# First attention: where VectorE splits the third part of the next quad's weights

## The chip, the cores and the metric

The kernel runs on one core of a Trainium2 chip. The metric is the device time of one execution in microseconds (us), lower is better. Five things work side by side in the core and meet only at semaphores: TensorE (PE for its matmuls, PEld for its weight loads), VectorE (DVE), ScalarE (ACT), GpSimd (POOL) and the sync engine (SP), which here only issues DMA transfers, one after the other in program order.

## The reference, cut to what matters

Input `x` is (4, 512, 256): four batches of 512 tokens of width 256. The model adds three blocks to it: a first causal self-attention with 16 heads of width 64, a cross attention with 16 heads of width 16, and a two-layer local transformer block. The change touches the first attention alone:

```python
xn = layernorm(x)
q = einsum('ahe,bce->bach', W_Q, xn)
k = einsum('ahe,bce->bach', W_K, xn)
v = einsum('ahe,bce->bach', W_V, xn)
scores = einsum('bach,baCh->bacC', k, q)
masked = where(causal, scores, -1e10)
attn = softmax(masked / sqrt(64), axis=-1)
z = einsum('bacC,baCh->bach', attn, v)
x = x + einsum('aeh,bach->bce', W_O, z)
```

## The kernel before, in words

**Units.** The first attention runs as 32 units, each one pair of heads of one batch. Eight units share one quad of heads (`QUNITS` is 8), and there are four quads (`QUADS` is 4). All engines run the same software pipeline of slots: the slot of unit `u` finishes unit `u` (transposes of the probabilities, weighted values), makes scores and softmax of unit `u + 1`, and projects k, q and v of unit `u + 2`. Slots are numbered `j` = 0 to 7 within a quad. A hardware loop (`Fori`) runs over the first three quads, eight slots in its body, and the last quad is written out behind it.

**Weights of a quad.** One DMA (`quad_weights`, line 514) brings 768 KB, the k, q and v weights of a quad, into one buffer `aw`. Matmuls run on rounded float32 operands and a rest: ScalarE rounds each of the three parts into `aw_hi` (line 783), VectorE writes the rest `aw_lo = aw - aw_hi` (`rest_of_weights_of_quad`, lines 1050 and 1051) and counts semaphore `a_lo` up by one for each part. During quad `c` the parts of quad `c + 1` are made: parts 0 and 1 in slot 5 of VectorE's order, part 2 (the v weights) in slot 6. Three things wait on `a_lo`: TensorE's projections (line 1510 for k and q, line 1520 for v, first used for the new quad at the end of slot 6), and SP, since `aw` may be overwritten only when all three rests are made.

**SP's queue.** SP issues for every unit four 128 KB transfers that copy the halves of the rounded k into both halves of `k2` (`other_half`, lines 551 to 555; the profile calls the tiles k and k_round). It first waits until ScalarE has rounded k (`k_hi`), and TensorE's first scores of the unit wait until all four have landed (`k_both`). Between the eighth unit of a quad and the first unit of the next one the same queue holds the wait for the split weights and the next load:

```python
            with sp.Fori(0, QUADS - 2) as c:
                for j in range(QUNITS):
                    other_half(c * QUNITS + j)
                sp.wait_ge(a_lo, 3 * c + 6)
                quad_weights(c + 2)
            for u in range(NU - 2 * QUNITS, NU):
                other_half(u)
```

This loop runs twice. The k of the unit whose `other_half` comes right behind `quad_weights` is rounded in slot 6, and its scores stand at the start of slot 7. At the start of the kernel the same sequence stands once in straight code: a wait for `a_lo` at 3, `quad_weights(1)`, `other_half(0)`.

**VectorE's slot.** In order: copy of the transposed probabilities 0 (`evac_pT`), masked scores of head 0 (three banks, line 1076, then `negmax`, line 1083), copy 2, masked scores of head 1, copy 4, the rest of k (lines 1065 and 1066), reciprocal of the softmax sums of head 0 (line 1088), reciprocal of head 1, the rest of q (lines 1058 and 1059), copy of z (line 1122). GpSimd multiplies the probabilities of a head by the reciprocal (line 658, four instructions for each head), and TensorE's transposes of head 0 of the next slot (line 1560) wait for the four of head 0.

Of the kernel before, what the change touches and what calls it, by code (L numbers as in the profile page):

```python
# [21 lines left out]
QUNITS = 2 * B  # L22
# [59 lines left out]
def build(nc, a, out, x2_dram):  # L82

    with ExitStack() as ctx:
# [199 lines left out]
        def use_z(u):  # L284
            return 5, 3 * u + 2 + B // 2
# [189 lines left out]
        def wait_full(eng, use):  # L475

            bank, n = use
            eng.wait_ge(full[bank], n + 1)
            return psum[bank]
# [544 lines left out]
        def _(dve):  # L1024
# [24 lines left out]
            def rest_of_weights_of_quad(c, i):  # L1049
                dve.wait_ge(a_hi, 3 * c + (i + 1))  # L1050
                dve.tensor_tensor(aw_lo[:, i], aw[:, i], aw_hi[:, i], ALU.subtract).then_inc(a_lo, 1)

            def rest_of_q(u):

                bank = wait_full(dve, use_q(u))
                dve.wait_ge(q_hi, u + 1)
                dve.tensor_tensor(q2[ADH:P, 0, :], bank[0:ADH, :], q2[0:ADH, 0, :], ALU.subtract)
                dve.tensor_tensor(q2[0:ADH, 1, :], bank[ADH:P, :], q2[ADH:P, 1, :], ALU.subtract)\
                    .then_inc(read[use_q(u)[0]], 1)  # L1060

            def rest_of_k(u):
                bank = wait_full(dve, use_k(u))
                dve.wait_ge(k_hi, u + 1)
                dve.tensor_tensor(k_rest[0:ADH, 0, :], bank[0:ADH, :], k_round[0:ADH, :], ALU.subtract)
                dve.tensor_tensor(k_rest[ADH:P, 1, :], bank[ADH:P, :], k_round[ADH:P, :], ALU.subtract)\
                    .then_inc(read[use_k(u)[0]], 1)

            def masked_scores(u, j, h):

                for k, blocks in enumerate(S_TILES):
                    bank = wait_full(dve, use_s(u, h, k))
                    pass_wait(dve, passed_v)
                    at = 0
                    for i in blocks:
                        ins = dve.tensor_tensor_reduce(  # L1076
                            probs[:, j % 2, h, TRI_AT[i]:TRI_AT[i + 1]], bank[:, at:at + TRI[i]],
                            causal[:, S - TRI[i]:S], 1.0, -3e38, ALU.add, ALU.max, rowmax[:, j % 2, h, i:i + 1])
                        at += TRI[i]
                    ins.then_inc(read[k], 1)  # L1080
                for k in range(3):
                    wait_read(dve, use_s(u, h, k))
                dve.tensor_scalar(negmax[:, j % 2, h, :], rowmax[:, j % 2, h, :], -ADH ** -0.5, None, ALU.mult)\  # L1083
                    .then_inc(s_neg, 1)

            def inverse_sums(u, j, h):
                dve.wait_ge(s_exp, 2 * u + (h + 1))
                dve.reciprocal(rden[:, j % 2, h, :], den[:, j % 2, h, :]).then_inc(s_rden, 1)  # L1088

            def evac_pT(u, n):  # L1090

                h, k = divmod(n, 3)
                bank = wait_full(dve, use_t(u, h, k))
                at = KEYB_AT[T_TILES[k][0]]
                w = sum(KEYB[j] for j in T_TILES[k])
                dve.tensor_copy(pT[:, h, at:at + w], bank[:, 0:w]).then_inc(read[use_t(u, h, k)[0]], 1)

            def attention_slot(u, j, ahead, z, c=None):

                evac_pT(u, 0)  # L1100
                if ahead >= 1:
                    masked_scores(u + 1, j + 1, 0)
                if c is not None and j == QUNITS - 2:
                    rest_of_weights_of_quad(c, 2)
                evac_pT(u, 2)
                if ahead >= 1:
                    masked_scores(u + 1, j + 1, 1)
                evac_pT(u, 4)
                if ahead >= 2:
                    rest_of_k(u + 2)  # L1110
                if ahead >= 1:
                    inverse_sums(u + 1, j + 1, 0)
                if c is not None and j == QUNITS - 3:
                    rest_of_weights_of_quad(c, 0)
                if ahead >= 1:
                    inverse_sums(u + 1, j + 1, 1)
                if ahead >= 2:
                    rest_of_q(u + 2)
                if c is not None and j == QUNITS - 3:
                    rest_of_weights_of_quad(c, 1)  # L1120
                bank = wait_full(dve, use_z(u))
                dve.tensor_copy(z, bank[:, :]).then_inc(read[use_z(u)[0]], 1)
# [37 lines left out]
            with dve.Fori(0, QUADS - 1) as c:  # L1160
                for j in range(QUNITS):
                    z = zT[:, j // 2, :, :].rearrange("p k s -> p (k s)")[:, bass.ds((c * 2 + j % 2) * S, S)]
                    attention_slot(c * QUNITS + j, j, 2, z, c + 1)
            for j in range(QUNITS):
                attention_slot(NU - QUNITS + j, j, QUNITS - 1 - j, zT[:, j // 2, PAIRS - 2 + j % 2, :])
# [777 lines left out]
```

## Time and profile before

| | before |
|---|---|
| median of 3 runs | 1221.88 us (1221.18 to 1222.47) |
| profiled execution | 1221.09 us |
| its span in the trace | 1219.2 us |
| TensorE matmuls busy | 1158.6 us (95%) |
| VectorE busy | 843.6 us (69%) |
| ScalarE busy | 686.5 us (56%) |
| GpSimd busy | 592.3 us (49%) |

All times in the trace count from the start of the span. The first attention lies in the first third of it, and the slots 5, 6 and 7 of the first quad lie at 99 to 136 us. In a timeline a row gives the start, the duration, the engine, the line, the operation with output and inputs, the shapes and a count; in brackets stands how long the engine was idle before it, and what ended that. "In the timeline of SP" rows are DMA issues: the time on the row is the issue, not the transfer.

### The profile page before, as it was taken

The numbers are of one execution on the slowest core, as the hardware profiler recorded it, in microseconds if no ns is written. First come the engines' busy times: TensorE is split into PE (matmuls) and PEld (weight loads), VectorE is DVE, ScalarE is ACT, GpSimd is POOL, SyncE is SP. The second block draws the span as 40 slices with busy tenths as digits, with TensorE's granted clock in tenths as the row PEclk, the third lists the DMA queues.
The fourth block names the chain that finished last, engine by engine and source line by source line (L and its number), as shares of the span: only waits on it lengthen the run. The fifth ranks groups of instructions, "written<-read, shape, count | busy, mean of one in ns | idle before, by whom it ended". The sixth has DMA issues, their size and how long they took to land.

```text
span 1219.2 us, 20487 instructions
## 1 busy us (share of the span) xinstructions
PE 1158.6 (95%) x6672; PEld 887.5 (73%) x6672; DVE 843.6 (69%) x2443; ACT 686.5 (56%) x1696; POOL 592.3 (49%) x648
## 2 busy tenths in 40 slices
PE   5899999999999899998789999999999999999998
PEld 4677777787777776666567787777777778777676
DVE  7777778787877356688999567777675876664541
ACT  2667576667667223453567646647475565573821
POOL 2354544445453322148886664655655646562630
PEclk9999999999999999999999999999999999999999
DMA  7122121312121400010021000000001000002000
GB/s 233 40 49 74 41 52 35 78 35 52 35 53 47 162 18 18 1 61 33 3 89 43 1 1 18 1 1 1 1 18 46 29 2 1 1 5 66 19 27 26
DMA packets 31628, 46.11 MB, mean 38 GB/s; under 512 B 4572, under 2 KB 19632, under 8 KB 31536
## 3 DMA queue, kind: packets, MB, share of 16 engines
q1 hardware_dynamic: 31536, 44.98, 12.9%
q8 instruction: 45, 0.74, 0.3%
q14 instruction: 47, 0.39, 0.1%
HBM read 24.00 MB, written 4.19 MB: 23 GB/s over the span
## 4 chain that ended last, share of the span: by engine, by line
PE 56%; issue 20%; POOL 14%; DVE 7%; ACT 3%; DMA 0%; POOLq 0%; DVEq 0%; ACTq 0%
PE psum L1494 34%; POOL probs L658 14%; PE psum L1754 5%; PE psum L1803 5%; PE psum L1788 4%; PE psum L1770 4%; PE psum L1736 2%; ACT hnT_hi L974 1%; DVE lp L1353 1%; DVE ra L1309 1%; ACT hnT L974 1%; DVE rb L1315 1%; PE psum L1816 1%; DVE ss L1319 1%; DVE stats L1027 1%
## 5 line engine op out<-in xcount | busy, mean ns | idle before, releaser
L658 POOL TENSOR_TENSOR probs<-probs,rden 128x128 f32<-128x128 f32 (+3 forms) x256 | 177.6, 730 | 211.2 <-DVE rden L1088 211.2
L813 ACT ACTIVATE probs<-probs,negmax 128x128 f32<-128x128 f32 (+3 forms) x256 | 140.6, 554 | 22.6 <-DVE negmax L1083 22.6
L944 ACT ACTIVATE lp<-lp,lneg,rn 128x256 f32<-128x256 f32 (+1 forms) x256 | 143.8, 571 | 14.1 <-DVE lneg L1365 13.9
L1076 DVE CUSTOM_DVE_ANT_0 probs<-psum,causal 128x512 f32<-128x512 f32 (+3 forms) x256 | 110.0, 486 | 2.2 <-issue 0.8
L702 POOL TENSOR_TENSOR rn<-ss,neg_half 128x8 f32<-128x8 f32 x64 | 106.5, 1664 | 3.8
L1353 DVE CUSTOM_DVE_ANT_0 lp<-psum,local 128x256 f32<-128x256 f32 (+1 forms) x256 | 84.0, 384 | 25.6 <-PE psum L1754 25.6
L693 POOL TENSOR_TENSOR lp<-lp,lrden 128x768 f32<-128x768 f32 x64 | 95.0, 1484 | 0.0
L1494 PE MATMUL psum<-q,k_rest 128*128 128x256 f32 (+2 forms) x256 | 88.8, 358 | 4.3 <-DVE rowmax L1076 2.9
L1560 PE MATMUL psum<-ident,probs 128*128 128x128 f32 x640 | 91.0, 274 | 1.7 <-POOL probs L658 1.6
L1494 PE MATMUL psum<-w,hid 114*128 114x256 f32 (+1 forms) x384 | 85.5, 379 | 1.1 <-DVE hid L1421 1.1
L1494 PE MATMUL psum<-wqkv_hi,hT_lo 128*128 128x512 f32 x192 | 82.1, 428 | 4.1 <-DVE rb L1315 2.8
L690 POOL TENSOR_TENSOR lp<-lp,lrden 128x128 f32<-128x128 f32 x64 | 26.7, 418 | 118.7 <-DVE lrden L1370 118.7
L698 POOL TENSOR_TENSOR ra<-ra,rb 128x512 f32<-128x512 f32 x32 | 41.0, 1281 | 84.8 <-DVE rb L1315 84.7
L1494 PEld LDWEIGHTS psum<-w,hid 114*128 114x128 f32 (+1 forms) x384 | 72.2, 190 | 11.7 <-DVE hid L1421 1.7
L778 ACT ACTIVATE pT<-psum 128x512 f32<-128x512 f32 (+1 forms) x96 | 49.3, 514 | 55.3 <-PE psum L1560 55.3
L1560 PEld LDWEIGHTS psum<-ident,probs 128*128 128x128 f32 x640 | 74.2, 141 | 6.9 <-POOL probs L658 2.1
L1494 PE MATMUL psum<-hnT_lo,w_hi 128*114 128x512 f32 (+1 forms) x192 | 78.8, 411 | 0.0
L1494 PE MATMUL psum<-q,k 128*128 128x256 f32 (+2 forms) x256 | 78.8, 325 | 0.0
L1576 PE MATMUL psum<-pT,v 128*64 128x256 f32 (+3 forms) x512 | 76.0, 439 | 2.3 <-ACT pT L778 1.7
L931 ACT ACTIVATE sq<-psum 128x512 f32<-128x512 f32 x64 | 38.1, 598 | 70.6 <-PE psum L1494 64.3
L1421 DVE SCALAR_TENSOR_TENSOR hid<-psum,b,gl 114x512 f32<-114x512 f32 (+1 forms) x48 | 36.0, 750 | 59.5 <-PE psum L1494 46.8
L1494 PE MATMUL psum<-wqkv_hi,hT_hi 128*128 128x512 f32 x192 | 76.3, 397 | 0.0
(166 smaller groups left out, 3053.5 us busy)
## 6 DMA issues: line engine op xcount, KB each, us to landing
k<-k_round SPq DMA_DIRECT2D x128, 128.0 KB, 2.3
x<-in_x SPq DMA_DIRECT2D x8, 512.0 KB, 6.3
aw<-in_w_quads SPq DMA_DIRECT2D x4, 768.0 KB, 4.9
w_raw<-in_w SPq DMA_DIRECT2D x2, 1364.0 KB, 7.2
ctxT<-in_ctxT SPq DMA_DIRECT2D x4, 512.0 KB, 3.6
x_scratch<-x SPq DMA_DIRECT2D x4, 512.0 KB, 3.3
x<-x_scratch SPq DMA_DIRECT2D x4, 512.0 KB, 5.5
wqkv_raw<-in_wqkv SPq DMA_DIRECT2D x1, 1536.0 KB, 10.0
```

The source lines that it names most:

```text
L658: ins = pool.tensor_tensor(pr, pr, rden[:, j % 2, h, i:i + 1].broadcast_to([P, TRI[i]]), ALU.mult)
L693: pool.tensor_tensor(pr, pr, r, ALU.mult).then_inc(l_prob, 1)
L702: pool.tensor_tensor(rn[:, m % 2, t, i, :], ss[:, i, :], neg_half[:, 0:FH], ALU.pow).then_inc(l_rn, 1)
L813: ins = act.activation(pr, pr, ACT.Exp, bias=negmax[:, j % 2, h, i:i + 1], scale=ADH ** -0.5, accum_out=den[:, j % 2, h, i:i + 1])
L944: ins = act.activation(pr, pr, ACT.Exp, bias=lneg[:, u % 2, h, w:w + 1], scale=rn[:, m % 2, w, 0, 2 * j + h:2 * j + h + 1], accum_out=lden ...
L1076: ins = dve.tensor_tensor_reduce(probs[:, j % 2, h, TRI_AT[i]:TRI_AT[i + 1]], bank[:, at:at + TRI[i]], causal[:, S - TRI[i]:S], 1.0, -3e38 ...
L1353: ins = dve.tensor_tensor_reduce(lp[:, u % 2, h, lo:hi], bank[:, at:at + hi - lo], local[:, LOC - (hi - lo):LOC], 1.0, -3e38, ALU.add, ALU ...
L1494: ins = mm(dst, lhsT, rhs, start=i == 0, stop=i == len(pairs) - 1, **kw)
L1560: ins = pe.transpose(bank[:, at:at + P], probs[:, j % 2, h, lo:lo + P], ident[:, :])
L1576: ins = mm(bank[rows, c * P:S], v[:, b % 2, c, cols], pT[:, h, KEYB_AT[c]:KEYB_AT[c] + KEYB[c]], start=c == 0, stop=c == T - 1)
L1754: ins = mm(pair[h][:, at:at + n].rearrange("p (w k) -> p w k", k=P), lqT[rows, c, d, :], keys[rows], start=True, stop=True)
L1803: ins = mm(bank[:, i * D:(i + 1) * D], loT[:, FPAIRS - 1 - k, t * P:(t + 1) * P], wo[:, k, :], start=i == 0 and k == 0, stop=i == 1 and k ...
```

## The change

In VectorE's `attention_slot`, slot 6 (`j == QUNITS - 2`) of the first three quads, the call that splits part 2 is taken from its place behind the masked scores of head 0 and put behind the reciprocal of head 0 (and behind the split of part 0, which is made in slot 5 only). The number of instructions is the same, and no other engine's code is changed.

```diff
@@ -1100,8 +1100,6 @@
                 evac_pT(u, 0)
                 if ahead >= 1:
                     masked_scores(u + 1, j + 1, 0)
-                if c is not None and j == QUNITS - 2:
-                    rest_of_weights_of_quad(c, 2)
                 evac_pT(u, 2)
                 if ahead >= 1:
                     masked_scores(u + 1, j + 1, 1)
@@ -1112,6 +1110,8 @@
                     inverse_sums(u + 1, j + 1, 0)
                 if c is not None and j == QUNITS - 3:
                     rest_of_weights_of_quad(c, 0)
+                if c is not None and j == QUNITS - 2:
+                    rest_of_weights_of_quad(c, 2)
                 if ahead >= 1:
                     inverse_sums(u + 1, j + 1, 1)
                 if ahead >= 2:
```

## Rows read from the trace of the kernel before

**Rows 1.** TensorE's timeline, slots 5 to 7 of the first quad: start, duration, work, idle.

```profile
99.13 0.60 PE L1560 MATMUL psum<-ident,probs 128*128 128x128 f32 x4
...
114.37 0.50 PE L1494 MATMUL psum<-q,k_rest 128*128 128x512 f32 x1 [0.38 <-DVE rowmax L1076]
...
122.28 0.38 PE L1494 MATMUL psum<-aw_hi,xnT_lo 128*128 128x256 f32 x1
...
123.79 0.60 PE L1560 MATMUL psum<-ident,probs 128*128 128x128 f32 x4
124.22 0.47 PE L1494 MATMUL psum<-q,k_rest 128*128 128x512 f32 x1
...
135.50 0.60 PE L1560 MATMUL psum<-ident,probs 128*128 128x128 f32 x4
```

**Rows 2.** VectorE's timeline of the same stretch, around the three splits.

```profile
105.52 0.69 DVE L1096 COPY pT<-psum 128x512 f32<-128x512 f32 x1 [0.47 <-PE psum L1560]
...
107.54 0.18 DVE L1088 RECIPROCAL rden<-den 128x4 f32<-128x4 f32 x1
107.63 0.66 DVE L1051 TENSOR_TENSOR aw_lo<-aw,aw_hi 128x512 fp32r<-128x512 f32 x1
...
115.59 0.69 DVE L1051 TENSOR_TENSOR aw_lo<-aw,aw_hi 128x512 fp32r<-128x512 f32 x1
...
118.51 0.69 DVE L1096 COPY pT<-psum 128x512 f32<-128x512 f32 x1
...
120.53 0.18 DVE L1088 RECIPROCAL rden<-den 128x4 f32<-128x4 f32 x1
121.43 0.18 DVE L1088 RECIPROCAL rden<-den 128x4 f32<-128x4 f32 x1 [0.72 <-ACT probs L813]
```

**Rows 3.** SP's timeline at 90 to 130 us: DMA issues around the quad's load.

```profile
116.47 0.35 SPq L514 DMA_DIRECT2D aw<-in_w_quads  x1
118.97 2.39 SPq L554 DMA_DIRECT2D k<-k_round  x4
```

**Rows 4.** DMA issues at 118.9 to 121.5 us: KB each, median us to landing.

```profile
k<-k_round SPq DMA_DIRECT2D x4, 128.0 KB, 2.4
```

**Rows 5.** The load issued at 116.4 to 117.4 us: KB, us to landing.

```profile
aw<-in_w_quads SPq DMA_DIRECT2D x1, 768.0 KB, 4.1
```

**Rows 6.** SP's timeline at the kernel's start, where load and k transfers follow directly.

```profile
18.74 0.33 SPq L514 DMA_DIRECT2D aw<-in_w_quads  x1
19.29 1.17 SPq L554 DMA_DIRECT2D k<-k_round  x2
```

**Rows 7.** DMA issues at 18.7 to 22 us: KB each, median us to landing.

```profile
aw<-in_w_quads SPq DMA_DIRECT2D x1, 768.0 KB, 5.4
k<-k_round SPq DMA_DIRECT2D x4, 128.0 KB, 4.5
```

**Rows 8.** TensorE's timeline at 20 to 44 us: two long waits.

```profile
25.76 0.47 PE L1494 MATMUL psum<-q,k_rest 128*128 128x512 f32 x1 [0.62 <-DMA k<-k_round]
...
37.79 0.36 PE L1494 MATMUL psum<-aw_hi,xnT_lo 128*128 128x256 f32 x1 [4.46 <-DVE k_rest L1066]
```

**Rows 9.** Two windows: busy us (count) of each engine, granted clock, DMA share, GB/s.

```profile
38.30:41.70 3.40, 3.40 (x16) 3.29 (x15) 1.29 (x3) 0.60 (x1) 0.89 (x1) 0.50 0.02 5
550.30:553.70 3.40, 3.40 (x10) 2.63 (x9) 2.56 (x7) 0.60 (x1) 3.22 (x4) 0.50 0.00 0
```

**Rows 10.** TensorE's timeline at 540 to 553 us, its longest wait there.

```profile
549.88 0.50 PE L1494 MATMUL psum<-wqkv_hi,hT_lo 128*128 128x512 f32 x1 [2.56 <-DVE rb L1315]
```

**Rows 11.** GpSimd's timeline, first instruction of a unit: slot 4, then slot 5.

```profile
96.08 0.40 POOL L658 TENSOR_TENSOR probs<-probs,rden 128x128 f32<-128x128 f32 x1 [6.25 <-DVE rden L1088]
...
107.80 0.76 POOL L658 TENSOR_TENSOR probs<-probs,rden 128x128 f32<-128x128 f32 x1 [6.25 <-DVE rden L1088]
```

**Rows 12.** Weight loads' timeline: first transposes of slot 6.

```profile
111.03 0.42 PEld L1560 LDWEIGHTS psum<-ident,probs 128*128 128x128 f32 x4 [0.22 <-issue]
```

## The prediction

> **What bounds the kernel now.** I read TensorE's timeline of the slots around the change first. Its first transposes start slot 5 at 99.13 us, slot 7 at 123.79 and the next quad's slot 0 at 135.50 [rows 1]. Slot 7 takes 11.71 us and shows no wait: the matmuls of a slot run back to back, so in the first attention TensorE sets the pace, and every wait it gets is time of the kernel. Slots 5 and 6, which hold the splits, take 24.66 us together, 1.24 us more than two plain slots. The visible part of that is where TensorE waits in slot 6 for the masked scores (0.38 us at 114.37, more on single weight loads) [rows 1]; it comes before part 2 is split at 115.59 [rows 2], so part 2 does not cause it. Parts 0 and 1, which the change leaves alone, do.
>
> Then VectorE's timeline: where does part 2 lie now? In slot 5, a plain slot at this point, the copy of transposes 4 starts after 0.47 us of waiting for TensorE (105.52). In slot 6 the same copy starts at 118.51 with no wait [rows 2]. So the split of 0.69 us fills a gap of 0.47 us that would be there anyway, and VectorE is late by at most the difference, 0.22 us, because of it; and the second reciprocal of slot 6 waits 0.72 us for ScalarE again, so even that lateness ends on VectorE itself.
>
> Last, SP's timeline, since SP waits for this split. At 116.47, 0.88 us after the split's start, it issues the 768 KB load of the quad after next; only at 118.97 do the four k transfers of the next unit follow, because k is rounded only then [rows 3]. SP had time to spare: 2.5 us between the two.
>
> **The change, part by part.**
>
> *What it takes away.* 0.69 us of VectorE behind the masked scores of head 0, three times. Worth: nothing to 0.22 us each, since the wait for transposes 4 comes back in its place, and the wait for ScalarE behind it stays. I take 0.
>
> *What it adds on VectorE.* The split stands behind the first reciprocal. In slot 5 this very arrangement runs with part 0: reciprocal at 107.54, split at 107.63 for 0.66 us. In slot 6 the first reciprocal starts at 120.53 and the second at 121.43, after 0.72 us of waiting for ScalarE's exponentials [rows 2]. The split would run from 120.62 to 121.28 and fit into the gap with 0.15 us to spare. The second reciprocal, the rest of q and the copy of z stay where they are. TensorE's v projection for the new quad waits for part 2 too; it starts at 122.28 [rows 1], 1.0 us after the split's new end. That cover holds. Cost on VectorE: 0.
>
> *What it adds on GpSimd.* GpSimd starts its multiplications just behind the first reciprocal, and now beside the split. In slot 5 that is so today: the first instruction took 0.76 us instead of 0.40 in slot 4, which has no split [rows 11]. The delay of 0.36 us passes through the four instructions of head 0, for which the first transposes of the next slot wait. After slot 5 they show 0.22 us of waiting (111.03) [rows 12]. From the first reciprocal of slot 5 (107.54) to these transposes it was 3.49 us, with GpSimd as the one waited for. The same distance behind the reciprocal at 120.53 [rows 2] puts the transposes of slot 7 at 124.02 instead of 123.79 [rows 1], 0.23 us later. Bounds: 0, if they keep today's time, and 0.36. I take 0.2. The Trainium skill (SBUF — State Buffer, Who interferes with whom) says that a VectorE instruction with both inputs in SBUF and a GpSimd instruction that reads SBUF exclude each other, and the later one blocks until the first is done. By that rule the delay would be from 107.80, GpSimd's start, to the split's end, 108.29, which is 0.49 us; the row shows 0.36, and the sum would grow by 0.1 us per quad.
>
> *What it moves on SP.* This is the large term. The split's start moves from 115.59 to 120.62, by 5.0 us, and SP's wait with it. The load is then issued at 120.62 + 0.88 = 121.50 in place of 116.47. SP works in order: the four k transfers, ready to go at 118.97, are now held behind the wait and behind the load. They were done in time by little. Four issues take 2.39 us (to 121.36) and a transfer lands 2.4 us after its issue [rows 3, 4], so the last one landed at about 123.2; the scores of slot 7 that need it start at 124.22 [rows 1]. That is a slack of 1.0 us against a shift of some 5.
>
> How late do they land? The start of the kernel shows the same sequence with nothing between load and k transfers: load issued at 18.74, first k transfer at 19.29 [rows 6], the load landed after 5.4 us and the k transfers after 4.5 instead of 2.4 [rows 4, 7], and TensorE's scores, which had waited 0.62 us for exactly these transfers, started at 25.76 [rows 8], 7.02 us after the load's issue. Applied to 121.50 this gives scores at 128.52 and a wait of 128.52 - 124.22 = 4.3 us. The other way to add it up: the load alone lands after 4.1 us [rows 5], at 125.6, and the four transfers follow it on the same 16 engines at 0.6 us each (their spacing in the 2.39 us), which is 128.0, and with 0.2 us for the semaphore (as from the split's end at 116.28 to SP's issue at 116.47) 128.2, a wait of 4.0 us. I take 4.1. The lower bound is the case in which the load doesn't disturb them: first k issue at 121.50 + 0.55 = 122.05, last one 1.8 us later, landed 2.4 us behind it at 126.25, scores at 126.45, a wait of 2.2 us.
>
> How often: SP's loop runs over two quads only. The third time the part is split, no load and no wait stand in SP's queue. So this costs 2 x 4.1 = 8.2 us. In these two slots the 0.2 us from GpSimd vanishes inside the longer wait (transposes stand ahead of the scores); it counts once, in the third quad.
>
> *TensorE's clock.* A wait of 4.1 us can lower the clock. This trace has 4.46 us of waiting up to 37.79, and at 38.30 the granted clock was 0.50 (1.2 GHz, the lower of the two levels) for 3.4 us; and 2.56 us of waiting up to 549.88, with 0.50 from 550.30 for 3.4 us [rows 8, 9, 10]. At half the clock with TensorE busy throughout, 3.4 us hold 1.7 us less work. Bounds: 0 and 1.7 us for each of the two waits. I take 1.4, nearer to the upper one, since both long waits of the trace had it, and part of the slow stretch can fall into the wait itself. Cost 2 x 1.4 = 2.8 us.
>
> **Sum.** 0 + 0 + 8.2 + 2.8 + 0.2 = 11.2 us. Against the profiled execution (1221.09, span 1219.2) that is 1232.3 with a span of 1230.4; against the median of the runs, 0.8 us higher, 1221.9 + 11.2 = 1233.1 us. Nothing gives it back: every later slot of TensorE is as full as before, and the stages behind the first attention start later by the same amount.
>
> **The rivals.**
>
> *A. Held back, but hardly disturbed.* The k transfers wait for SP but not for the load's data, and the clock stays up: 2 x 2.2 + 0.2 = 4.6 us, 1226.5 us; with one or two clock drops up to 1230. For it: the load needs few of its microseconds on the engines, and transfers overlap. Against it: the 4.5 us to landing at the start. The Trainium skill (DMA: Bandwidth & Descriptors, Queues, rings and completion order) has a rule that leans to this rival, that a later transfer may finish its write before an earlier one, since data descriptors carry no barrier; and one that leans against it, that each engine takes the descriptors of one queue in order. By the first alone the time would be that of this rival. At the start the first k transfers did land before the load (issued 0.55 us later, 4.5 against 5.4 us to landing), but still 2.1 us later than undisturbed. Chance 0.19.
>
> *B. Hidden.* The change doesn't reach TensorE through SP: the scores of slot 7 don't need these four transfers so early, or SP's wait is passed earlier than I read. Then 0.2 x 3 = 0.6 us from GpSimd is left, 1222.5 us. Against it stands the order of the queue itself and the wait at 25.76. Chance 0.06.
>
> *C. Not slower.* VectorE's lateness in slot 6 is what holds TensorE, and taking 0.69 us out of the middle of it lets the masked scores of head 1 and all behind them come earlier; this decides if the extra 1.24 us of slots 5 and 6 can be won back. Price: 0.6 x 3 = 1.8 us for the split alone, 1220.1 us; all of it, 3.7 us, 1218.2 us. It needs B's condition as well, or the 8 us bury it. Against it: TensorE's waits lie ahead of the split, and behind it there are none. Chance 0.04.
>
> *D. Worse.* The waits grow beyond the start's example (both of SP's re-entries into its loop add time, the clock drops for more than one stretch each): above 1236.5 us. Chance 0.04.
>
> **How the numbers follow.** The forecast of the text has 0.67, with a range of its own from 2 x 4.0 + 0.2 = 8.2 us without any clock loss (1230.1) to 2 x 4.3 + 2 x 1.7 + 0.2 = 12.2 (1234.1), and about 2 us above for a second slow stretch. The predicted time is 1233.1 us. The range that should hold it 8 times in 10 takes in most of A and stops at D: 1227.5 to 1236.5 us. A measurement of this kernel can tell some 0.2% (2.4 us) from no change. Slower by more than that: forecast, A and D, 0.67 + 0.19 + 0.04 = 0.90, and 0.01 of what is left of B; 0.91. Faster by more than that: the larger half of C, 0.03. Within: B and the rest of C, 0.06.
>
> **What would show it right or wrong.** In SP's timeline of the changed kernel the load should be issued at about 121.5 us and the k transfers right behind it, at about 122.1, with 4 us or more to landing. TensorE's timeline should show a wait of about 4 us for the DMA of k ahead of the scores of slot 7, in the first and the second quad and not in the third; the third should show some 0.2 us ahead of the first transposes. GpSimd's first instruction beside the split should take 0.76 us in place of 0.40. The granted clock should be 0.50 for some 3.4 us near 128 us and near 230 us. VectorE's second reciprocal should keep its distance to the first one (0.9 us), and the v projection should not wait. If the scores wait 2 us and not 4, A holds and the sum of the DMA term was wrong; if there is no wait, B; if the clock stays at 1.00, the term of 2.8 us falls.

## The result, and the profile after

The changed kernel takes 1232.14 us (median of 6 runs, 1231.56 to 1234.76), the kernel before in the same runs 1222.10 us. The ratio is 1.0088, with an interval of 1.0075 to 1.0101: 10 us slower, 9.2 to 12.3 by the interval. Forecast were 1233.1 us and a range of 1227.5 to 1236.5. The profiled execution took 1231.56 us with a span of 1229.7, 10.5 us above the span of before.

The same number of instructions ran, and the busy times on the profile's page are those of before within 2.7 us (PEld 890.2 for 887.5, PE 1160.7 for 1158.6). The last two lines are one row of the page, of the changed kernel and then of before:

```profile
span 1229.7 us, 20487 instructions
...
PE 1160.7 (94%) x6672; PEld 890.2 (72%) x6672; DVE 844.4 (69%) x2443; ACT 686.5 (56%) x1696; POOL 592.7 (48%) x648
...
L1494 PE MATMUL psum<-q,k_rest 128*128 128x256 f32 (+2 forms) x256 | 90.0, 363 | 12.5 <-DMA k<-k_round 8.4
L1494 PE MATMUL psum<-q,k_rest 128*128 128x256 f32 (+2 forms) x256 | 88.8, 358 | 4.3 <-DVE rowmax L1076 2.9
```

The idle time in this row is what is new: of 12.5 us in place of 4.3 ahead of the matmuls of the scores, 8.4 are put down to the k transfers. The waits of TensorE at 50 to 420 us (us in total, times, longest) say that in the slots it is two waits (the rest is the one at the kernel's start [rows 8]):

```profile
PE psum L1494 <- DMA k<-k_round: 7.7, 2, 3.9
```

**SP.** Its timeline answers to [rows 3]: the load goes out at 121.55 us in place of 116.47, and the four k transfers, ready at 119, follow it at 122.32.

```profile
121.55 0.35 SPq L514 DMA_DIRECT2D aw<-in_w_quads  x1
122.32 17.44 SPq L554 DMA_DIRECT2D k<-k_round  x8
```

**Landing.** The DMA issues at 121.4 to 124.9 us (KB, median us to landing) answer to [rows 4, 5], and look like those of the kernel's start [rows 7]: 5.1 us for the load in place of 4.1, 4.5 for each k transfer in place of 2.4. In the second quad they are 5.6 and 4.7 us.

```profile
aw<-in_w_quads SPq DMA_DIRECT2D x1, 768.0 KB, 5.1
k<-k_round SPq DMA_DIRECT2D x4, 128.0 KB, 4.5
```

**TensorE.** Its timeline in slot 7 of the first quad, of the second and of the third. The scores start at 128.57 and 230.45 after waiting for the DMA; in the third quad, where SP has nothing to load, there is no such wait. These rows answer to [rows 1]; the last two lines are the scores of slot 7 in the second and the third quad of the kernel before.

```profile
124.11 0.65 PE L1560 MATMUL psum<-ident,probs 128*128 128x128 f32 x4
128.57 0.50 PE L1494 MATMUL psum<-q,k_rest 128*128 128x512 f32 x1 [3.80 <-DMA k<-k_round]
...
230.45 0.80 PE L1494 MATMUL psum<-q,k_rest 128*128 128x512 f32 x1 [3.92 <-DMA k<-k_round]
...
328.36 0.65 PE L1560 MATMUL psum<-ident,probs 128*128 128x128 f32 x4
328.79 0.47 PE L1494 MATMUL psum<-q,k_rest 128*128 128x512 f32 x1
...
220.45 0.47 PE L1494 MATMUL psum<-q,k_rest 128*128 128x512 f32 x1
...
316.69 0.47 PE L1494 MATMUL psum<-q,k_rest 128*128 128x512 f32 x1
```

**The clock.** Two windows of the changed kernel (busy us and count of each engine, granted clock, DMA share, GB/s). The granted clock was 0.50 from 129.7 for 3.4 us, and from 228.7, while TensorE still waited, for 6.8 us; the kernel before has no such stretch between 42 and 550 us.

```profile
129.70:133.10 3.40, 3.40 (x15) 3.21 (x14) 2.59 (x11) 1.79 (x6) 0.00 (x0) 0.50 0.01 2
228.70:235.50 6.80, 5.05 (x18) 4.67 (x19) 2.40 (x11) 1.40 (x5) 0.00 (x0) 0.50 0.07 18
```

**VectorE and GpSimd.** VectorE's timeline in slot 6 answers to [rows 2], GpSimd's to [rows 11]. The wait for the transposes before copy 4 is back (0.46 us), the split fits between the reciprocals, with 0.20 us of waiting for ScalarE left of 0.72, and GpSimd's first instruction takes 0.76 us, where in slot 6 of the kernel before it took 0.40 (at 120.78).

```profile
118.59 0.69 DVE L1096 COPY pT<-psum 128x512 f32<-128x512 f32 x1 [0.46 <-PE psum L1560]
120.61 0.18 DVE L1088 RECIPROCAL rden<-den 128x4 f32<-128x4 f32 x1
120.70 0.66 DVE L1051 TENSOR_TENSOR aw_lo<-aw,aw_hi 128x512 fp32r<-128x512 f32 x1
121.57 0.18 DVE L1088 RECIPROCAL rden<-den 128x4 f32<-128x4 f32 x1 [0.20 <-ACT probs L813]
...
120.87 0.76 POOL L658 TENSOR_TENSOR probs<-probs,rden 128x128 f32<-128x128 f32 x1 [6.65 <-DVE rden L1088]
```

**Where the time went.** The copies of z (line 1122), one at the end of each of the 32 slots, measure it. These are the ones of slots 6 and 7 in the first two quads, before and then after:

```profile
124.01 0.69 DVE L1122 COPY zT<-psum 128x512 f32 x1
...
135.72 0.69 DVE L1122 COPY zT<-psum 128x512 f32 x1
...
220.24 0.69 DVE L1122 COPY zT<-psum 128x512 f32 x1
...
231.95 0.69 DVE L1122 COPY zT<-psum 128x512 f32 x1
```

```profile
124.15 0.69 DVE L1122 COPY zT<-psum 128x512 f32 x1
...
141.35 0.69 DVE L1122 COPY zT<-psum 128x512 f32 x1
...
225.91 0.69 DVE L1122 COPY zT<-psum 128x512 f32 x1
...
243.97 0.69 DVE L1122 COPY zT<-psum 128x512 f32 x1
```

The shifts here and below are rounded only at the end, so the rows give them within 0.01 us. Against before the copies stand at +0.14 us at slots 5 and 6 of the first quad (an offset that arises in slot 5, ahead of the moved split), +5.63 at slot 7, +5.68 at slot 6 of the second quad, +12.02 at its slot 7, +11.92 and +11.97 around slot 7 of the third, and +12.01 at the last slot. So two slots cost 5.49 and 6.34 us, of which some 0.1 us comes back in the slot after the second, and the third costs 0.05. At the scores the shift was 4.21 us in the first quad (128.57 - 124.22 - 0.14) and 4.32 in the second; the rest of each slot, 1.28 and 2.02 us, lies behind the wait.

The shift stays at 12.0 us through the later stages and then falls to 10.5. VectorE's instructions of line 1421 (the last transformer stage), first before, then after, at two places:

```profile
1074.00 0.75 DVE L1421 SCALAR_TENSOR_TENSOR hid<-psum,b,gl 114x512 f32<-114x512 f32 x1 [0.90 <-ACT gl L983]
...
1190.30 0.75 DVE L1421 SCALAR_TENSOR_TENSOR hid<-psum,b,gl 114x512 f32<-114x512 f32 x1 [2.23 <-PE psum L1494]
```

```profile
1086.01 0.75 DVE L1421 SCALAR_TENSOR_TENSOR hid<-psum,b,gl 114x512 f32<-114x512 f32 x1 [0.90 <-ACT gl L983]
...
1200.78 0.75 DVE L1421 SCALAR_TENSOR_TENSOR hid<-psum,b,gl 114x512 f32<-114x512 f32 x1 [2.23 <-PE psum L1494]
```

Between them the kernel before has a stretch at half the clock, and the changed one, at the same work 12 us later, has none:

```profile
1137.40:1140.80 3.40, 3.40 (x13) 2.30 (x13) 1.98 (x11) 3.40 (x12) 0.00 (x0) 0.50 0.00 0
```

```profile
1149.00:1152.40 3.40, 3.40 (x20) 2.43 (x21) 2.40 (x11) 3.40 (x12) 0.23 (x1) 1.00 0.00 0
```

### The profile page after: what moved, and what is told of

Same layout as the page of the kernel before. It is cut to its first block, busy times and chain, and to the rows that moved or that the text cites. A ratio compares the mean times of both kernels' runs of the same rounds, so it can differ in the third digit from the quotient of the medians.

```text
span 1229.7 us, 20487 instructions
## 1 busy us (share of the span) xinstructions
PE 1160.7 (94%) x6672; PEld 890.2 (72%) x6672; DVE 844.4 (69%) x2443; ACT 686.5 (56%) x1696; POOL 592.7 (48%) x648
## 4 chain that ended last, share of the span: by engine, by line
PE 55%; issue 20%; POOL 14%; DVE 7%; ACT 3%; DMA 0%; POOLq 0%; DVEq 0%; ACTq 0%
PE psum L1494 34%; POOL probs L658 14%; PE psum L1754 5%; PE psum L1803 5%; PE psum L1788 4%; PE psum L1770 4%; PE psum L1736 2%; ACT hnT_hi L974 1%; DVE lp L1353 1%; DVE ra L1309 1%; ACT hnT L974 1%; DVE rb L1315 1%; PE psum L1816 1%; DVE ss L1319 1%; DVE stats L1027 1%
## 5 line engine op out<-in xcount | busy, mean ns | idle before, releaser
L1494 PE MATMUL psum<-q,k_rest 128*128 128x256 f32 (+2 forms) x256 | 90.0, 363 | 12.5 <-DMA k<-k_round 8.4
```

The lines of the kernel that those rows point to most:

```text
L1494: ins = mm(dst, lhsT, rhs, start=i == 0, stop=i == len(pairs) - 1, **kw)
```

## The experiments

Theory Q is the one of the prediction: SP's queue holds the k transfers behind the late wait and the load, and the clock falls in TensorE's wait. Its rival, V, is that the split's new place on VectorE, beside GpSimd and ScalarE, costs the time.

### SP's order: k transfers first

```diff
+            other_half(0)
             with sp.Fori(0, QUADS - 2) as c:
-                for j in range(QUNITS):
+                for j in range(1, QUNITS + 1):
                     other_half(c * QUNITS + j)
                 sp.wait_ge(a_lo, 3 * c + 6)
                 quad_weights(c + 2)
-            for u in range(NU - 2 * QUNITS, NU):
+            for u in range(NU - 2 * QUNITS + 1, NU):
```

On top of the change:

> The changed kernel, with SP's queue reordered: the k transfers of the next quad's first unit are issued ahead of the wait for the split weights and the load, in place of behind them. Theory Q (the cost is SP's queue: load and k transfers held behind the late split, and the clock that falls in the wait): the k transfers go out at about 119 us again, the scores of slot 7 find them landed, TensorE has no DMA wait and no clock drop near 130 and 230 us, and the time is that of before, 1222 us (1221 to 1223). Theory V (the cost is the split's place on VectorE beside GpSimd and ScalarE, and the DMA wait only comes along): the split stands where the change put it, so the time stays at 1232 us.

Measured: 1221.30 us, ratio to before 1.0001 (0.9991 to 1.0010). SP's timeline shows the k transfers at 119.39 and the load at 122.08, and TensorE has no DMA wait in the first attention:

```profile
119.39 2.39 SPq L554 DMA_DIRECT2D k<-k_round  x4
122.08 0.35 SPq L514 DMA_DIRECT2D aw<-in_w_quads  x1
```

V falls: the split stands where the change put it, and the 10 us are gone.

On top of the kernel before, the same edit alone:

> The kernel before (split at its old place) with the k transfers of the next quad's first unit issued ahead of the wait and the load. Beside the first experiment it leaves the move on VectorE alone, without SP: both should have the same time within 0.2 us for each quad; here the transposes of slot 7 should start without the wait for GpSimd (0.2 us). Time 1221 to 1222 us.

Measured: 1221.32 us, ratio 0.9999 (0.9989 to 1.0008). Taken together the two leave the move on VectorE and GpSimd by itself. By the copies of z, slot 7 lost 0.07, 0.06 and 0.09 us in the three quads with the moved split, and nothing (0.01 at most) without it: 0.2 us in all, too little to show in the medians (1221.30 and 1221.32).

### A late load with the split at its old place

```diff
                 sp.wait_ge(a_lo, 3 * c + 6)
+                sp.wait_ge(s_rden, 2 * QUNITS * c + 2 * QUNITS)
                 quad_weights(c + 2)
```

On top of the kernel before:

> The kernel before, split at its old place; SP alone waits longer: before the load it also waits for the second reciprocal of slot 6 (which ends at about 121.6 us, 0.3 us after the split's end in the changed kernel). Theory Q: the load goes out at about 121.8, the scores of slot 7 wait some 4.2 us and a little more (4.5) in two quads, the clock falls, and the time is 1232 to 1234 us although VectorE's order is that of before. Theory V: 1222 us.

Measured: 1233.91 us (four executions), ratio 1.0105 (1.0088 to 1.0122). VectorE splits at 116.92, at its old place in a trace that runs 1.3 us late from the start; SP's load goes out at 123.11:

```profile
116.92 0.69 DVE L1052 TENSOR_TENSOR aw_lo<-aw,aw_hi 128x512 fp32r<-128x512 f32 x1
...
123.11 0.35 SPq L514 DMA_DIRECT2D aw<-in_w_quads  x1
```

TensorE's waits at 50 to 420 us:

```profile
PE psum L1495 <- DMA k<-k_round: 8.5, 2, 4.6
```

Slot 7 ends 5.25 and 6.00 us later, 1.13 and 1.27 more than the shift at its scores, and the granted clock was 0.50 for 3.4 us in each, from 129.4 and from 231.8. The loss is made without touching VectorE, by SP's late issue alone. Q holds in both directions.

### The load without its data

```diff
-                quad_weights(c + 2)
+                sp.dma_start(aw[:, 0, 0, 0:4], a["w_quads"][c + 2][:, 0, 0, 0:4]).then_inc(ld_aw, 16)
```

On top of the change; all else, SP's waits too, as there. The kernel leaves out nearly all of the third and fourth quads' weights, and computes these quads with old ones:

> The changed kernel with the loads of the third and fourth quads' weights cut to 2 KB (four columns of the k part); this leaves out the rest of those weights, so these two quads are computed with old ones, at the same cost. SP's order and waits stay. Data theory D (half of the wait is the load's 768 KB ahead of the k transfers on the same engines): the k transfers go out at 122.2 to 124 us, land 2.4 us after issue, and the wait for them falls from 3.9 (and 0.2 of latency) to about 2.2 us each; with the clock drops perhaps gone, 1226 to 1229 us. Order theory O (the load's bytes don't matter, the late issue does it all): the wait stays near 3.8 us and the time at 1232 us.

Measured: 1225.90 us, ratio 1.0037 (1.0025 to 1.0050). The issues at 122 to 126 us, and TensorE's timeline in slot 7 of the first two quads:

```profile
k<-k_round SPq DMA_DIRECT2D x4, 128.0 KB, 2.3
aw<-in_w_quads SPq DMA_DIRECT2D x1, 2.0 KB, 1.7
```

```profile
127.02 0.50 PE L1494 MATMUL psum<-q,k_rest 128*128 128x512 f32 x1 [1.72 <-DMA k<-k_round]
...
225.08 0.50 PE L1494 MATMUL psum<-q,k_rest 128*128 128x512 f32 x1 [1.52 <-DMA k<-k_round]
```

With SP just as late but no data in the way, the waits are 1.7 and 1.5 us, slot 7 ends 2.05 and 1.84 us later than before (not 5.5 and 6.3), and the clock stays at 1.00 through both. The scores shift by 2.12 and 1.94 us. So of the shift of 4.2 us at the scores about one half is the late issue, and the other half the 768 KB ahead of the k transfers. Theory D held, O fell. This was the case on which the prediction's rival A rested; it is real, and it needs the load to be gone.

### Half the move

```diff
                 if ahead >= 1:
                     masked_scores(u + 1, j + 1, 1)
+                if c is not None and j == QUNITS - 2:
+                    rest_of_weights_of_quad(c, 2)
                 evac_pT(u, 4)
```

Part 2 split here, and at neither of the other places:

> The split of part 2 stands between its two places: behind the masked scores of head 1, ahead of the copy of transposes 4. It starts at about 117.9 us, the load goes out at 118.8, just when k is ready (118.95), so the k transfers follow it at 119.5. Theory Q with data ahead of k: scores of slot 7 at 118.8 + 7.0 = 125.8, a wait of 1.6 us (1.3 by adding transfer times) in two quads, mostly without a clock drop: 1225 us (1224 to 1227). If only the order of issue counted, the k transfers would land at 124.0 and nothing would be lost: 1222 us.

Measured: 1223.55 us, ratio 1.0018 (1.0009 to 1.0028). SP's timeline and TensorE's in slot 7:

```profile
118.86 0.35 SPq L514 DMA_DIRECT2D aw<-in_w_quads  x1
```

```profile
126.05 0.50 PE L1494 MATMUL psum<-q,k_rest 128*128 128x512 f32 x1 [1.62 <-DMA k<-k_round]
...
223.94 0.50 PE L1494 MATMUL psum<-q,k_rest 128*128 128x512 f32 x1 [1.49 <-DMA k<-k_round]
```

The scores start 7.2 us after the load's issue, and 7.0 in the changed kernel (121.55 to 128.57), as at the kernel's start [rows 6, 8]. Slot 7 ends 1.70 and 1.54 us later, with no clock drop behind the waits. Half the move costs a quarter to a third of the whole: waits of 1.5 and 1.6 us cost about their own length, those of 3.8 and 3.9 cost more.

### The wait filled with matmuls

```diff
                     wait_read(pe, use_k(u))
+                    if fill:
+                        bank = wait_free(pe, use_s(u, 0, 0))
+                        for _ in range(fill):
+                            mm(bank[:, :], aw_hi[:, 0, 0, 0:P], xnT_hi[:, 0, 0, :], start=True, stop=True)
                     pe.wait_ge(k_both, K_DMAS * u + K_DMAS)
```

On top of the change, with `fill` at 12 in slot 7 of the looped quads:

```profile
124.51 3.04 PE L1541 MATMUL psum<-xnT_hi,aw_hi 128*128 128x512 f32 x12
128.30 0.50 PE L1495 MATMUL psum<-q,k_rest 128*128 128x512 f32 x1 [0.74 <-DMA k<-k_round]
```

```profile
128.30:135.00 6.70, 6.70 (x42) 5.95 (x43) 5.00 (x21) 4.18 (x13) 0.00 (x0) 1.00 0.01 4
```

The granted clock stayed at 1.00 behind both waits. Slot 7 lost 3.87 and 4.01 us in the first two quads, against 5.49 and 6.34 in the changed kernel, so the clock costs 1.6 and 2.3 us by this comparison (1.3 and 2.0 by the shifts within the changed kernel; the transfers landed 0.2 to 0.3 us earlier here). With the clock up, the end of slot 7 moved 0.1 us less than its scores. The third quad lost 2.85 us, the matmuls themselves. In the medians it is no gain: 1232.75 us (two executions), ratio 1.0091 (1.0074 to 1.0108). In the trace the third quad pays 2.8 of the 4.0 us that the first two save, and the rest is lost behind it: the granted clock was 0.50 for 3.4 us from 423.4, where the changed kernel has 1.00, and the shift against before grew there from 11.0 to 12.5 us. Whether the added matmuls have a part in that drop is not shown.

### A better order

On top of the change, SP's order of the first experiment, and part 1 split in slot 6 in place of slot 5:

```diff
                 if ahead >= 1:
                     masked_scores(u + 1, j + 1, 0)
+                if c is not None and j == QUNITS - 2:
+                    rest_of_weights_of_quad(c, 1)
                 evac_pT(u, 2)
...
-                if c is not None and j == QUNITS - 3:
-                    rest_of_weights_of_quad(c, 1)
                 bank = wait_full(dve, use_z(u))
```

> The changed kernel with the k transfers ahead of the load in SP's queue, and part 1 split in slot 6 (where part 2 was before) in place of the end of slot 5. Theory: parts 0 and 1 in slot 5 make VectorE late for the masked scores of slot 6, for which TensorE waits; part 1 has 0.8 us of it, and in slot 6 it is hidden as part 2 was. So 0.8 us less in each of three quads, 1.24 us of excess over plain slots falling to about 0.4: 2.4 us faster than before, 1219 us. If ScalarE's own lateness in slot 5 holds TensorE instead, there is no gain: 1221 to 1222 us.

Measured: 1219.69 us against 1221.46, ratio 0.9984 (0.9975 to 0.9992). It is the fastest kernel here, 1.8 us below the one before, somewhat less than the 2.4 expected; SP's order alone had given nothing (1221.30 and 1221.32 above). The weight loads of TensorE in slot 6 show what it gained; in this trace the wait for the masked scores is 0.22 us where three waits of 0.61, 0.18 and 0.26 stood in the kernel before:

```profile
114.96 0.19 PEld L1495 LDWEIGHTS psum<-q,k_rest 128*128 128x128 f32 x1 [0.22 <-DVE rowmax L1077]
```

By the copies of z each quad gains 0.8 us in slot 5 and gives about 0.1 back in slot 6 and another 0.1 in slot 7, and the first quad another 0.25 in the slot behind; at the end of the first attention 1.7 us are left. What takes these parts back is open. Its profiled execution has a span of 1215.3 us, which flatters it: it lacks the clock drop that before has at 550 us, and 2.2 of its 3.9 us come from there.

## Why the prediction was right

*SP's queue, twice.* Right, and in its working too. The split's start moved by 5.1 us (120.70), the load went out 0.85 us behind it as forecast (121.55 for 121.50), and the k transfers behind it. Scores were forecast at 128.5 by the kernel's start and at 128.2 by adding transfers; they came at 128.57. I had taken 4.1 us for each wait, between the two; measured at the scores were 4.21 and 4.32, so 8.5 for 8.2 us. The start's example was the better of the two estimates. What the sum of transfers left out is visible in the landing times: load and k transfers slow each other, 5.1 us for 4.1 on the load. The Trainium skill's rule that each engine takes the descriptors of one queue in order (DMA: Bandwidth & Descriptors, Queues, rings and completion order) fits the trace: the k transfers landed 4.4 to 4.6 us after their issue behind the load, and 2.3 behind the load without its data. The same section's other rule, that a later transfer may finish its write before an earlier one, made little difference: in the first quad the first k transfer landed 0.3 us behind the load (122.32 + 4.6 = 126.9, 121.55 + 5.1 = 126.6), in the second 0.3 us ahead of it (223.87 + 4.7 = 228.6, 223.31 + 5.6 = 228.9), and TensorE waited 3.8 and 3.9 us. The distance from the load's issue to the scores was not fixed either: 7.0 and 7.1 us in the changed kernel, 7.2 and 7.1 in the kernel with half the move, 6.6 and 7.2 with the late load.

*The third quad.* Right: no load, no wait for a DMA.

*The clock.* Right in kind, low in size: 1.4 us taken for each, 1.3 to 1.6 and 2.0 to 2.3 measured, so 3.3 to 3.9 for 2.8 us. In the first quad the clock fell 1.1 us behind the end of the wait and the slot paid most of 1.7 us. In the second it fell during the wait and stayed at 0.50 for 6.8 us, of which 5.05 were busy. The upper bound of 1.7 us for each wait did not hold: it came from two examples in which the slow stretch was 3.4 us, and I had read that as its length. Even behind the wait of 4.46 us [rows 8], which all traces have, the stretch was 6.8 us in three of them (both kernels with the reordered queue alone, and the late load) and 3.4 in the other six.

*GpSimd.* The mechanism held (0.76 us for 0.40), and the first transposes of slot 7 waited 0.22 us, as after slot 5 [rows 12]. The rows put this wait down to "issue" and not to GpSimd, as the prediction reads it; but the transposes start 0.12 us behind the end of GpSimd's fourth instruction in both places (110.91 to 111.03 before, 123.98 to 124.10 after). The end of the slot moved by only 0.05 us in the third quad, and 0.2 us over three quads in the comparison of the two reordered kernels. At the scores of the third quad it was still 0.17 us (328.79 against 316.69 + 11.93); where in slot 7 the rest of it is taken up is open. The first instruction was 0.36 us longer here too, and not the 0.49 us that full exclusion by the Trainium skill (SBUF — State Buffer, Who interferes with whom) would give by the prediction's estimate; the profile's times on GpSimd are rough, so these rows do not decide against the rule.

*VectorE.* Right: the wait for transposes 4 came back (0.46 us), the second reciprocal kept its time, and the v projection did not wait.

*"Nothing gives it back."* Wrong for the profiled execution. The sum for the first attention was 11.2 us; the three slots cost 11.9, and with the offset of slot 5 the shift behind it was 12.0. Of that, 1.5 us went again in the last transformer stage, where the kernel before falls to half the clock at 1137 us and the changed one doesn't. Nothing shows that the change did this: the changed kernel with the added matmuls, whose shift there is 12.5 us, has the drop, and so has the one with the late load. In the profiled execution the forecast's 11.2 us lie close to the measured 10.5 partly by luck, since terms that were 0.7 us too small together and one that was left out lie on opposite sides. The other five executions of the changed kernel had a mean granted clock of 0.990 or 0.991, the profiled one 0.993, so they may well have had the drop; how the 10.0 us between the medians divide is not shown.

*Rival A* would have been right if the load had no data: its two waits of 2.2 us were 2.12 and 1.94 at the scores there. *B* fell with SP's and TensorE's timelines, *C* with the two reordered kernels, in which the moved split gained nothing and cost 0.2 us.

## What to carry to other kernels

A step that is moved on one engine takes its semaphore along: look at every queue that waits for that count, and at what is issued behind the wait in that queue, even if it has nothing to do with the step. Here 0.7 us of hidden work was moved from one gap to another at no cost on their own engine, and it cost 10 us through a load for which nobody was in a hurry, but which stood ahead of four small transfers with 1 us of slack. Here, with the urgent, small transfers ahead of the large, patient one, the place of the split is free within 0.2 us; it can then be used to unburden the slot where TensorE does wait.

## What the runs showed of the hardware that was not expected

A wait of TensorE can cost well over its own length, and not in proportion: waits of 1.5 to 1.7 us moved the slot's end by 1.5 to 2.1 us (four of them, no clock drop behind them), waits of 3.8 to 4.6 us had a stretch at half the clock behind or in them in all four cases of the changed kernel and of the late load, and moved the slot's end by 5.3 to 6.3 us. That stretch was 3.4 us long three times and 6.8 us once. One and the same wait does not always have the same effect: the wait of 2.56 us near 550 us [rows 10] stands in all nine traces, and has a stretch at half the clock at or behind it in seven of them (not in those of the load without its data and of the better order). And the span of a single profiled execution of this kernel moves by 1.5 to 2.2 us with clock drops that come or stay out far from any edit (at 550 and 1137 us), so that shifts at fixed places of the trace are better than the two spans for telling what an edit did.
